# One layer norm in place of two in a row, and the second batch's context measured in the prologue: the first two attentions of a four-layer kernel

## The reference

```python
x = x + _L0_xattn_ref(_layernorm(x), ctx_1024, cos, sin, ln_lat_g, ..., bo)
x = x + _L0_ffn_ref(_layernorm(x), ...)
x = x + _L1_xattn_ref(ctx_1024, _layernorm(x), gamma_x, beta_x, gamma_l, beta_l, ...)
...
def _layernorm(x, axis=-1, eps=1e-05):
    return (x - mean) / sqrt(var + eps)
```

## Time and profile before

| What | us |
|---|---|
| median of the three runs | 2627.6 |
| the profiled execution's own time | 2621.09 |
| its span (first to last instruction) | 2619.0 |
| PE busy | 2164.3 (83%) |
| DVE busy | 1372.9 (52%) |
| ACT busy | 768.1 (29%) |
| POOL busy | 738.6 (28%) |

### The profile page before, as it was taken

The page is one execution under the profiler, slowest core; times in us unless marked ns, Lnnn a source line. Parts: engine busy times, 40 slices in busy tenths (PEclk is TensorE's granted clock), DMA queues, the critical chain, the costliest instruction groups (busy, mean ns, idle before and its releaser), DMA issues.

```text
span 2619.0 us, 35664 instructions
## 1 busy us (share of the span) xinstructions
PE 2164.3 (83%) x14376; PEld 1559.9 (60%) x14376; DVE 1372.9 (52%) x2170; ACT 768.1 (29%) x1182; POOL 738.6 (28%) x784
## 2 busy tenths in 40 slices
PE   5899999489957889886978885898688886688984
PEld 3566665379834444436965553898444543588883
DVE  7899998432267776764224444222765563411113
ACT  4455544022123333331222331001244444111111
POOL 4223222134321001101333221565311110255543
PEclk8899999699979999997986996899699998699996
DMA  3011100368700000003650001897000000288872
GB/s 112 25 28 30 33 21 17 115 225 300 255 18 9 9 11 19 9 1 125 238 171 15 19 9 50 286 326 246 28 13 15 11 3 19 106 282 276 289 267 92
DMA packets 91123, 269.95 MB, mean 103 GB/s; under 512 B 13424, under 2 KB 38768, under 8 KB 90576
## 3 DMA queue, kind: packets, MB, share of 16 engines
q0 software_dynamic: 46512, 210.66, 23.6%
q1 hardware_dynamic: 44448, 57.02, 7.1%
HBM read 239.84 MB, written 15.20 MB: 97 GB/s over the span
## 4 chain that ended last, share of the span: by engine, by line
PE 60%; DVE 16%; issue 6%; DMA 6%; POOL 5%; ACT 2%; SPq 1%; POOLq 0%; DVEq 0%; ACTq 0%
PE psum L2415 12%; PE psum L280 11%; PE psum L2438 8%; PE psum L876 6%; PE psum L896 5%; DVE plain L1868 4%; DMA plain<-in_l_en,plain 3%; PE psum L1656 3%; PE psum L1689 3%; PE psum L1706 2%; DVE plain L1082 2%; DVE plain L1109 2%; PE psum L318 1%; PE psum L1749 1%; POOL plain L2539 1%
## 5 line engine op out<-in xcount | busy, mean ns | idle before, releaser
L2415 PE MATMUL psum<-plain 128*128 128x128 f32 x3904 | 495.5, 280 | 6.0 <-DVE plain L2492 4.2
L2415 PEld LDWEIGHTS psum<-plain 128*128 128x128 f32 x3904 | 487.3, 196 | 17.8 <-DVE plain L2492 4.3
L280 PE MATMUL psum<-split 128*128 128x256 f32 (+1 forms) x1728 | 386.9, 379 | 69.9 <-DVE split L353 17.3
L280 PEld LDWEIGHTS psum<-split 128*128 128x128 f32 x1728 | 296.6, 215 | 181.3 <-issue 80.7
L2539 POOL DMA_INDIRECT plain<-in_l_ffn,plain x274 | 261.6, 955 | 418.8 <-PE psum L2438 280.9
L2438 PE MATMUL psum<-plain 128*128 128x256 f32 x1160 | 303.9, 385 | 40.3 <-DVE plain L2504 40.3
L1308 ACT ACTIVATE plain<-psum 128x1024 f32<-128x1024 f32 x224 | 226.1, 1024 | 280.7 <-PE psum L896 258.5
L1109 DVE TENSOR_TENSOR plain<-plain 128x1024 f32<-128x1024 f32 x200 | 278.2, 1391 | 20.9 <-PE psum L876 12.1
L2438 PEld LDWEIGHTS psum<-plain 128*128 128x128 f32 x1160 | 199.8, 192 | 61.5 <-DVE plain L2504 33.0
L1360 POOL TENSOR_TENSOR plain<-plain 128x512 f32<-128x512 f32 x48 | 78.2, 1629 | 558.1 <-DMA plain<-plain 553.5
L2504 DVE TENSOR_TENSOR plain<-plain,psum 128x256 f32<-128x256 f32 x198 | 81.3, 419 | 292.0 <-ACT plain L2463 291.7
(11 more groups left out here) (195 smaller groups left out, 2391.1 us busy)
## 6 DMA issues: line engine op xcount, KB each, us to landing
plain<-plain SPq DMA_DIRECT2D x192, 64.0 KB, 2.0
sorted_y<-plain SPq DMA_DIRECT2D x76, 128.0 KB, 4.8
plain<-in_l_w SPq DMA_DIRECT2D x20, 256.0 KB, 2.7
plain<-in_l_ffn,plain POOLq DMA_INDIRECT x274, 6.1
plain<-in_ctx SPq DMA_DIRECT2D x8, 512.0 KB, 5.4
tokens_x<-plain SPq DMA_DIRECT2D x4, 1024.0 KB, 4.8
plain<-in_l_wo SPq DMA_DIRECT2D x28, 128.0 KB, 2.1
plain<-in_l_tab SPq DMA_DIRECT2D x3, 1024.0 KB, 5.0
```

Of the source, the lines that this page charges most:

```text
L280: m = t.e.matmul(out, lhs[x], rhs[y], start=(first and n == 0), stop=(last and n == 2), skip_group_check=skip)
L2415: m = t.e.matmul(K.bank(b)[:, 256 * z + P * f:256 * z + P * f + P], ws[:, f, c0:c0 + 128], xt[:, k, :], start=(f == 0 and k == 0 and z == ...
```

## The change

The two norms of the latents become one: the statistics of `x` are taken once, and POOL's root is that of `var * (1 + eps) + eps * eps`, which is what two norms in a row amount to. The second statistics, the second root and the second scaling go, in layer 0's prologue, in layer 1's prologue and in layer 1's side work. `XL[0]` moves to the place that `XL[1]` has, which frees the place of the second context; its two loads are issued with the first ones, at the end of SP's starting list, and its statistics are taken in the prologue, by DVE after the first query's low part and by POOL after the bias. The scaling of both halves is then one piece of side work where there were two, each with its statistics. The lists of weights lose one piece each (0.4 in layer 0, 0.3 in layer 1). ACT's wait for the turned latents before the first exponentials now holds in layer 0 too, since the first sum lies where `XL[0]` now is.

The diff, without functions that only lose a parameter or are deleted as unused:

```diff
-        self.XL = [self.STAGE8[1], view(15616, 2048, "p (t d) -> p t d", d=D)]
+        self.XL = [view(15616, 2048, "p (t d) -> p t d", d=D)] * 2
...
-def gpsimd_stats(g, K, lo, hi):
+def gpsimd_stats(g, K, lo, hi, twice=False):
     g.wait_ge("bn_aggr", g.next("bn_aggr", hi - lo))
     g.before_next()
-    g.e.tensor_scalar(K.VE[:, lo:hi], K.MV[:, lo:hi, 1], EPS, None, ALU.add).then_inc(*g.up("var_eps"))
+    if twice:
+        m = g.e.tensor_scalar(K.VE[:, lo:hi], K.MV[:, lo:hi, 1], 1.0 + EPS, EPS * EPS, ALU.mult, ALU.add)
+    else:
+        m = g.e.tensor_scalar(K.VE[:, lo:hi], K.MV[:, lo:hi, 1], EPS, None, ALU.add)
+    m.then_inc(*g.up("var_eps"))
...
 def vector_pair(v, K, bt):
+    yield
     for h in range(2):
-        yield
-        vector_pair_stats(v, K, bt, h)
         vector_pair_scaled(v, K, bt, h)
     for h in range(2):
         yield
         vector_turn(v, K, K.C64, 2 * bt + h, K.gain["ctx"], K.TMP2)
...
-def vector_late_scaled(v, K, xn, gain):
+def vector_late_scaled(v, K, xn):
     for h in range(2):
         vector_scaled(v, K, K.X, xn, 4 * h, 4 * h + 4)
-        if gain:
-            v.wait_ge("normed", v.made["normed"])
-            vector_stats(v, K, xn, 4 * h, 4 * h + 4)
...
-def vector_late_turn(v, K, xn, gain, tmp):
-    for h in range(2):
-        if gain:
-            vector_scaled(v, K, xn, xn, 4 * h, 4 * h + 4)
+def vector_late_turn(v, K, gain, tmp):
     for h in range(2):
         vector_turn(v, K, K.XNT, h, gain, tmp)
...
             if n == 0 and own:
-                weights = weights + [0.3, 0.3, 0.3, 1.2]
+                weights = weights + [0.3, 0.3, 1.2]
...
             elif not own:
-                weights = [1.5, 1.5, 1.5, 0.0, 0.2, 0.0, 0.2, 0.2, 0.4, 0.4, 1.2, 1.2]
+                weights = [1.5, 1.5, 1.5, 0.0, 0.2, 0.0, 0.2, 0.2, 0.4, 1.2, 1.2]
...
         vector_stats(v, K, K.X, i, j)
         yield
         vector_scaled(v, K, K.X, K.XL[1], i, j)
-        v.wait_ge("normed", v.made["normed"])
-        vector_stats(v, K, K.XL[1], i, j)
-        yield
-        vector_scaled(v, K, K.XL[1], K.XL[1], i, j)
...
         split(0, 0)
         split(0, 1)
         query(0)
+        for h in range(2):
+            vector_pair_stats(v, K, 1, h)
         wsplit(1)
...
-                if own and n < 2:
+                if n < 2:
                     s.wait_ge("turned", K.at.get(("late", L, n), 0))
...
-        gpsimd_late_stats(g, K, True)
-        n = g.seen["normed"] - 8
+        gpsimd_late_stats(g, K)
+        n = g.seen["normed"]
         rope(0, 0)
         rope(0, 1)
         gpsimd_bias(g, K, n)
-        context = skip_first(gpsimd_pair(g, K, 1))
+        gpsimd_pair(g, K)
+        context = skip_first(iter([None] * 3))
...
-    if L == 0:
-        y.wait_ge("turned", K.at.get(("late", L, 1), 0))
-        sync_pair(y, K, 1)
...
     y.e.dma_start(K.BIAS, T["bc"][:, 0:256]).then_inc(*y.dma("bias"))
+    sync_pair(y, K, 1)
     for L in range(4):
```

More of the change, by code:

```diff
@@ L410, in sync_pair @@
         y.e.dma_start(K.STAGE8[bt][:, 4 * h:4 * h + 4, :], K.T["ctx"][bt, 512 * h:512 * h + 512].rearrange(
-            "(t p) d -> p t d", p=P)).then_inc(*y.dma(f"ctx{h}"))
+            "(t p) d -> p t d", p=P)).then_inc(*y.dma(f"pair{bt}{h}"))
 def vector_pair_stats(v, K, bt, h):
-    v.wait_ge(f"ctx{h}", v.next(f"ctx{h}", 16))
+    v.wait_ge(f"pair{bt}{h}", 16)
     vector_stats(v, K, K.STAGE8[bt], 4 * h, 4 * h + 4)
@@ L430, in vector_pair, with gpsimd_pair @@
         vector_turn(v, K, K.C64, 2 * bt + h, K.gain["ctx"], K.TMP2)
-def gpsimd_pair(g, K, bt):
+def gpsimd_pair(g, K):
     for h in range(2):
-        yield
         gpsimd_stats(g, K, 4 * h, 4 * h + 4)
         g.next("normed", 4)
-    for h in range(2):
-        yield
 def tensor_pair(t, K, bt, ring):
-    for h in range(2):
-        yield
+    yield
     for h in range(2):
@@ L465, in vector_late_stats, with gpsimd_late_stats @@
         vector_stats(v, K, K.X, 4 * h, 4 * h + 4)
-def vector_late_scaled(v, K, xn, gain):
+def vector_late_scaled(v, K, xn):
     for h in range(2):
         vector_scaled(v, K, K.X, xn, 4 * h, 4 * h + 4)
-        if gain:
-            v.wait_ge("normed", v.made["normed"])
-            vector_stats(v, K, xn, 4 * h, 4 * h + 4)
-def vector_late_turn(v, K, xn, gain, tmp):
-    for h in range(2):
-        if gain:
-            vector_scaled(v, K, xn, xn, 4 * h, 4 * h + 4)
+def vector_late_turn(v, K, gain, tmp):
     for h in range(2):
         vector_turn(v, K, K.XNT, h, gain, tmp)
[L484 to L497, removed]
-    for h in range(2):
[L499 to L505, removed]
+def gpsimd_late_stats(g, K):
+    for h in range(2):
+        gpsimd_stats(g, K, 4 * h, 4 * h + 4, True)
+    g.next("normed", 8)
 def gpsimd_bias(g, K, n):
@@ L519, in tensor_late @@
     for h in range(2):
-        t.wait_ge("normed", t.next("normed", 4) if gain else n - 4 + 4 * h)
+        t.wait_ge("normed", n - 4 + 4 * h)
         tensor_turn(t, K, xn, 4 * h, ring, gain)
@@ L820, in second @@
     def second():
-        for _ in range(4):
+        for _ in range(3):
             yield
@@ L1180, in first @@
         keys(0, 1)
-        vector_late_turn(v, K, K.XL[0], K.gain["lat"], K.TMP2)
+        vector_late_turn(v, K, K.gain["lat"], K.TMP2)
         split(0, 0)
@@ L1375, in normed @@
     def normed(h):
-        for _ in range(2):
-            gpsimd_stats(g, K, 4 * h, 4 * h + 4)
-            g.next("normed", 4)
-            yield
+        gpsimd_stats(g, K, 4 * h, 4 * h + 4, True)
+        g.next("normed", 4)
+        yield
     def second():
@@ L2970, in gpsimd_program @@
     g.wait_ge("filled", 1)
-    run(gpsimd_pair(g, K, 0), 1000)
+    gpsimd_pair(g, K)
     for L in range(4):
```

5 lines of the change are left out of this document (2 added, 3 removed).

## The result

The changed kernel takes 2603.32 us (median of 6 runs, 2592.36 to 2609.74) against 2625.91 for the kernel before (6 runs, 2619.18 to 2628.39). The ratio is 0.9915 with a 95% interval of 0.9889 to 0.9940, so it is faster by 0.6 to 1.1%. The traced execution took 2605.22 us.

What follows compares the result with a forecast made beforehand. PE was taken to bound the kernel (60% of the span), so gains count only where it stands still. 4.8 + 3.4 + 4.8 + 5.3 = 18.3 us off the three-run median 2627.6 gave 2609.3 us, range 2604.0 to 2615.5.

Steps and rivals of the forecast that it cites:

- Part 1: Layer 0's prologue: query and first scores 5.1 us earlier, less a 0.3 us wait at L1003; gain 4.8 us.
- Part 2: Side work of layer 0's first attention: normalising starts where the second context's measuring started; gain 3.4 us.
- Part 3: Layer 1's prologue: POOL's rotary work no longer waits for a second root; gain 4.8 us.
- rival (a): Clock takes part back: bursts after standstills meet 1.2 GHz, 1.5 us at each of three places, 2614 us; chance 0.12.
- Part 4: Layer 1's first attention, side work: transposes 4.8 us earlier, plus 0.5 us from running at 2.4 GHz; gain 5.3 us.
- (b): Layer 0's prologue: DVE's statistics beside POOL's bias additions cost 1.4 us, 2610.7 us; chance 0.07.
- (c): Layer 0's prologue: keys bound it if rotary work ends after 42 us, leaving about 1 us gain, 2613; chance 0.01.
- (d): All four places: other work sets PE's standstills, only Part 1 or Part 4 remains, 5 us, 2622.6; chance 0.03.
- (e): Layer 0's prologue: DVE waits for late second-context loads, holding attention 0; 2632 us if landing at 65; chance 0.02.

## Why the prediction was right and wrong

**Part 1, prologue of layer 0: 4.8 us, right in sum.** In the first pair of traces the first scores came 4.87 us earlier. Inside it two terms were off and partly cancel.

The query was 4.4 us earlier and not 5.1. ACT's last copy ended at 36.22 and not at 35.94, because the 36 matmuls ended at 30.25 (21.90 + 8.35) and not at 29.8. A window of the changed kernel shows PE slow for longer than before at the start of its work:

```profile
26.00:28.00 2.00, 2.00 (x11) 1.71 (x10) 0.25 (x1) 0.59 (x1) 0.00 (x0) 1.00 0.27 67
```

Both traces start six matmuls in 24 to 26 us; in 26 to 28 the changed kernel starts 11 and the kernel before 16. The granted clock of this trace reads 1.00 there from 20 us on and does not show it. Behind the last copy another 0.46 us were lost: the query follows it by 1.33 us instead of 0.87 (41.08 to 41.95), since the third turn ran beside POOL's rotary work and the fourth beside the bias. Here the prediction had POOL wrong: the rotary work was to end 1.2 us earlier, near 34.7, and it ended at 35.81 instead of 35.90. It waited for the swaps until 29.64 and then ran slower beside DVE's turns.

From the query to the first scores it was 5.97 us (43.52 less 37.55) and before 6.44 (48.39 less 41.95): PE had 0.89 granted in the window 40 to 44, and before 0.71 in the window 44 to 48, at about the same distance behind its query. This is luck of the pair: the other traces have 7.0 and 6.9 us without a change in layer 0, and 6.5 and 5.7 with the whole change. By three traces of each (for before its two and that of the single norm in layer 1), the first scores came at 49.1 and 43.6, 5.5 us earlier, and the second step's at 83.0 and 74.4, 8.6 earlier where 8.2 was forecast. The wait for L1003 was put at 0.3 and measured 0.3 (0.37 in the first trace). The statistics beside the bias cost nothing.

**Part 2: 3.4 us, right.** 3.38 in the experiment with the context alone, 3.36 in the change (10.84 to 7.48; 7.48 in all three traces of it, 10.84 in both of before).

**Part 3: 4.8 us, measured 4.1.** The mechanism holds to the detail: POOL starts after the one root, DVE pays 4.41 us beside it, the second transposes wait 1.23 for ACT. PE's first transposes gained the 4.8 us. Then 0.8 were given back, which is rival (a) at half its price: PE comes to the query sooner and is at the low clock for longer (0.61 granted in 722 to 724 us, before 0.83 in 742 to 744, each some 3 to 5 us behind the query's start).

**Part 4: 5.3 us, right,** with the half-microsecond of the clock: 59.9 to 54.5 or 54.6 in all eight traces that have this edit.

**The sum: 18.3 us, not refuted.** The product of the parts gives 0.9927, which is 19.1 us of 2621.1, and three comparisons of the whole give 0.9918 with 0.0017 either way.

**What failed is the range's term for the scatter of runs:** "less 1 us for the scatter of runs (1.6 between the outer ones)", and with it the base from which it subtracted, the median of three runs. Three runs that agree within 1.6 us said little. More runs of the same kernel spread over 21 to 29 us, and the median of before itself lay 10 to 14 us lower in the later comparisons. Already in the first comparison six runs of before have a median of 2625.91 and not 2627.6; with that base the lower end would have been 2602.3 and the measured time inside, so the 0.7 us of the miss are no finding about the change. Had the base been one of the later medians, the same 18.3 us would have given 2594.9 to 2599.3, below the stated range.

Of the rivals, (a) is seen as 0.8 us in part 3 and in no other place; (b), (c), (d) and (e) did not happen. Whether 2 or 3 us of surplus belong to the change stays open. For it speaks that the experts of layer 0 are 3.6 us shorter on the mean in seven traces than in six; against it, that no instruction there was changed, and that the interval of the whole holds the 18.3 us without them.

## What to carry to other kernels

Follow a standstill to the instruction that ends it and then to the queue it stands in. In layer 1 the gain was the whole chain from the first scaling to the second (4.8 us: a scaling of 1.4, statistics of 1.8, and 1.6 for the root on POOL), of which DVE's own work is two thirds. In layer 0's prologue 10.6 us of DVE's work went (7.0 of scalings, two rounds of statistics of 1.8), but the query came only 4.4 us earlier, because ACT's four gain and copy pairs stand there next. Work that moves ahead of a stall costs little if its new place has idle time in the row: 3.6 us of statistics in 3.41 us of idle time cost PE 0.3. And before giving a range for an absolute time, look at how far one unchanged kernel spreads over many runs; a difference of 0.7% is read more surely from the starts of the same matmul in several traces, and from several, not from one pair.

## What was not expected of the hardware

PE's clock changes at other moments in each execution of the same program, also where PE stands still for well under a microsecond between long runs of work (3.35 busy of 4 us, then 0.50 or 1.00 granted). The runs' times follow it: 2606.65 us at a mean of 0.895 and 2581.89 at 0.904 for one kernel. The granted clock at the very start of a trace need not be right: it read 1.00 in 26 to 28 us where 11 matmuls started instead of 16. In one of three traces of one kernel the experts of layer 2 took 5.9 us longer, in a stage that took 152.2 to 152.5 us in all the others. Batch statistics on DVE keep their time beside POOL's additions (1.40 us for four) where two-input operations nearly double (2.36 against 1.29).
